# Map scatters and attention gathers of a four-model graph network: counted by batch with up to 96 open, and no scatters in the graph's pass

## The chip, the core and the metric

The kernel runs on one core of one Trainium2 chip. The metric is the device time of one execution in microseconds; lower is better. All arithmetic is float32.

## The reference

Node rows `x` (50,000 x 128) and 25,000 edges (`src`, `dst`, sorted by `dst`) go through four graph networks one after the other. Each adds its result to `x` and normalizes the row. The first one has four attention layers, and it is the one that the change touches:

```python
h = x @ W
e = ea @ We
alpha = (h @ a_s)[src] + (h @ a_d)[dst] + e @ a_e
alpha = leaky_relu(alpha, 0.2)
alpha = segment_softmax(alpha, dst, N)
out = segment_sum(h[src] * alpha[:, None], dst, N) + b
x = (out - mean(out)) * rsqrt(var(out) + 1e-5) * gamma + beta
```

After it come a relation network of three layers, a neighbour-mean network of three layers and one tensor-product convolution, all on the same edges.

## The kernel before

The work is a sequence of passes, each a `Pass` with its own tiles and semaphores. At the end of a pass all five engines meet, GpSimd clears the pass's semaphores, and they meet again (lines 76 to 79). So a pass lasts until its last engine is done, and nothing of the next one starts earlier.

The 25,000 edges are padded to 25,088 and stand in 196 columns (`K`) of 128 edges. A gather or scatter by edge moves 128 rows, one for each partition, and is one indirect DMA that GpSimd (POOL) issues. The passes that matter here:

- **graph** (lines 744 to 950) works out for each edge which segment it is in and where its row goes. VectorE and TensorE do it in a chain of small steps, ScalarE stores the second half of a map from nodes to rows, SyncE (SP) stores the results. POOL runs the first 24 of 196 map scatters (`EARLY`), which wait until the whole map has landed (`self_mapped`). A map scatter writes four floats for each edge that ends a segment into the table `gat_rows0`.
- **dense0**, named `x` in the trace (lines 966 to 1049), takes 98 blocks of 512 nodes. SP loads `x`, TensorE transposes and multiplies, VectorE completes the row, SP stores 536 KB a block into the same table, in columns that the map scatters don't write. POOL runs the other 172 map scatters beside it.
- **p0** (`PlainLayers` with `FirstRows`): POOL first gathers 196 columns by `dst` (line 2406, through a ring of four slots), then 196 columns by `src` into the big tile `H` (`gather_rows`, line 2358). Meanwhile all nodes run through attention layers 1 to 3 as if they had no edges on the other engines, in 98 blocks (the plain stream). VectorE ends with the logits.
- **p1, p2, p3** (`plain_rows`): `gather_rows` again brings 196 columns from that layer's table (132 floats a row), beside a plain stream that takes a third of the 98 blocks through the networks that follow. The logits stand at the start of these.
- **soft** and **d** (line 1145 on) follow each of p0 to p3 and read `H`. They need all 196 columns.

`place_in_map` and `gather_rows` count what they have open with sixteen semaphores: DMA number `c` adds to semaphore `c % 16`. Before each sixteenth DMA they wait on all sixteen, that is until every DMA issued so far has landed. At the end they wait on all sixteen again.

Of the kernel before, what the change touches and what calls it, by code (L numbers as in the profile page):

```python
# [8 lines left out]
U32 = mybir.dt.uint32  # L9
# [20 lines left out]
R_DST, R_SRC, R_TYPE, R_SH, R_LEN, R_TE = 0, 1, 2, 4, 8, 24  # L30
MUL = 32
PEEL = 10
RING = 16


class Chain:
# [289 lines left out]
class Kernel:  # L326
# [29 lines left out]
    def build(self):  # L356
# [17 lines left out]
        with ExitStack() as ctx:  # L374
# [16 lines left out]
            with ExitStack() as gat:  # L391
                self.rend = gat.enter_context(nc.sbuf_tensor("rend", [P, K], F32))
                self.asad = gat.enter_context(nc.sbuf_tensor("asad", [P, K, 2], F32))
                self.prev01 = gat.enter_context(nc.sbuf_tensor("prev01", [HALF, 2, P], F32))
                self.head01 = gat.enter_context(nc.sbuf_tensor("head01", [HALF, 2, P], F32))
                self.next01 = gat.enter_context(nc.sbuf_tensor("next01", [HALF, 2, P], F32))
                self.carry01 = gat.enter_context(nc.sbuf_tensor("carry01", [HALF, 2, P], F32))
                self.pen_row = gat.enter_context(nc.sbuf_tensor("pen_row", [1, 2, K], F32))
                self.row01 = gat.enter_context(nc.sbuf_tensor("row01", [1, 2, K], F32))
                self.Wg = gat.enter_context(nc.sbuf_tensor("Wg", [P, 4, TW], F32))  # L400
                self.cg = gat.enter_context(nc.sbuf_tensor("cg", [P, 4, TW], F32))
                self.Gc = gat.enter_context(nc.sbuf_tensor("Gc", [P, D], F32))
                self.g3 = gat.enter_context(nc.sbuf_tensor("g3", [P, D], F32))
                with Pass(nc, "early") as early:
                    self.b3, self.mapv = early.sb("b3", [P, D]), early.sb("mapv", [P, KG, KT, 4])
                    self.flag, self.own_i = early.sb("flag", [1, 1], I32), early.sb("own_i", [P, C], I32)
                    self.mput, self.placed = early.sb("mput", [P, K], U32), early.sems("map_placed", RING)
                    self.self_map, self.self_mapped = early.sb("self_map", [P, NP // P, 4]), early.sem("self_map_stored")
                    self.weights, self.plain_constants = Weights(self, early), PlainConstants(self, early)
                    self.records()  # L410
                    self.order()
                    self.graph()
                    self.dense0()
                self.H = gat.enter_context(nc.sbuf_tensor("H", [P, K, T0W], F32))
                self.lt = gat.enter_context(nc.sbuf_tensor("logit_terms", [P, 2, K], F32))
                self.pw = gat.enter_context(nc.sbuf_tensor("pw", [P, K], F32))
                self.pl = gat.enter_context(nc.sbuf_tensor("pl", [P, K], F32))
                self.te2 = gat.enter_context(nc.sbuf_tensor("te2", [P, K], F32))
                first = 0
                for l in range(4):  # L420
                    if l == 0:
                        self.run("p0", lambda q: PlainLayers(self, q), lambda q: FirstRows(self, q))
                    else:
                        self.plain_rows(l, first, (self.NBLK - first) // (4 - l))
                        first += (self.NBLK - first) // (4 - l)
                    with ExitStack() as marks:
                        self.same = marks.enter_context(nc.sbuf_tensor(f"same_run{l}", [P, ND], U8))
                        self.soft(l)
                        self.slots(l)
# [314 lines left out]
    def graph(self):  # L744
# [3 lines left out]
        with Pass(self.nc, "graph") as q:  # L748
# [20 lines left out]
            pr, pc = q.ps("rows", 4), q.ps("cols")  # L769
            ld, ch, sbr, sbst, icst = q.sem("loaded"), q.sem("steps"), q.sem("marks_ready"), q.sem("marks_stored"), q.sem("rows_stored")  # L770
            fr, ft, fk = q.sem("fields_ready"), q.sem("fields_turned"), q.sem("fields_kept")
            er, et, cr, ct, ohr, mr = (q.sem(n) for n in ("ends_ready", "ends_turned", "carries_ready", "carries_turned", "kinds_ready", "map_rows_ready"))
            block = q.block()
            by_row = lambda ap: ap.rearrange("(g r p) -> r g p", g=2, p=P)

            pt, pa, pc_ = pr[:, 0, :], pr[:, 1, :], pr[:, 2, :]

            @block.gpsimd
            def _(pool):
                pool.wait_ge(mr, 1)  # L780
                pool.wait_ge(self.self_mapped, 16 * (self.G + 1))
                self.place_in_map(pool, 0, self.EARLY)

            @block.scalar
            def _(act):
# [71 lines left out]
            def _(v):  # L857
# [37 lines left out]
                v.wait_ge(ft, 1)  # L895
                v.tensor_scalar(self.src2_i[:, :], pf[0][:, K:2 * K], 2.0, 1.0, ALU.mult, ALU.add)
                v.tensor_copy(self.dst_i[:, :], pf[1][:, 0:K])
                v.tensor_scalar(self.mput[:, :], pf[1][:, K:2 * K], float(2 * T0W // 4), float((GB + MAP) // 4), ALU.mult, ALU.add).then_inc(mr, 1)
                v.tensor_copy(self.put_i[:, :], pf[1][:, K:2 * K])
                st.run(v.tensor_copy(self.rend[:, :], pf[2][:, 0:K]))  # L900
                v.sem_inc(fk, 1)
# [48 lines left out]
                v.tensor_copy(self.shareD[:, :], pf[2][:, 0:K])  # L950


    EARLY = 24

    def place_in_map(self, pool, first, end):

        pieces = self.t0w.rearrange("n (q w) -> (n q) w", w=4)
        bound = pool.to_reg(self.NP * 2 * T0W // 4 - 1)
        for c in range(first, end):
            if c and c % RING == 0:  # L960
                for j in range(RING):
                    pool.wait_ge(self.placed[j], c // RING * 16)
            pool.indirect_dma_start(pieces, bass.IndirectOffsetOnAxis(self.mput[:, c:c + 1], 0), self.mapv[:, c // KT, c % KT, :], None,  # L963
                                    bounds_check=bound, oob_is_err=False).then_inc(self.placed[c % RING], 16)

    def dense0(self):

# [2 lines left out]
        with Pass(self.nc, "x") as q:  # L970
# [25 lines left out]

            @block.gpsimd
            def _(pool):
                self.place_in_map(pool, self.EARLY, K)
                for j in range(RING):  # L1000
                    pool.wait_ge(self.placed[j], len(range(j, K, RING)) * 16)

            @block.tensor
            def _(pe):
# [1343 lines left out]
def gather_rows(kn, pool, got, table, index, rows, width, before=()):  # L2348

    K, bound = kn.K, pool.to_reg(rows - 1)  # L2350
    for c in range(K):
        if c == K - 8 * KT:
            for s, n in before:
                pool.wait_ge(s, n)
        if c and c % RING == 0:
            for j in range(RING):
                pool.wait_ge(got[j], c // RING * 16)
        pool.indirect_dma_start(kn.H[:, c, 0:width], None, table, bass.IndirectOffsetOnAxis(index[:, c:c + 1], 0),  # L2358
                                bounds_check=bound, oob_is_err=False).then_inc(got[c % RING], 16)
    for j in range(RING):  # L2360
        pool.wait_ge(got[j], len(range(j, K, RING)) * 16)


class FirstRows(Stream):


    def __init__(self, kn, q):
# [1 line left out]
        self.dg = kn.H[:, kn.K - 8 * KT:kn.K, :].rearrange("p c w -> p (c w)").rearrange("p (r k w) -> p r k w", r=4, k=KT)  # L2369
        self.heads_kept, self.attr_kept = q.sem("heads_kept"), q.sem("attr_kept")  # L2370
        self.gate = q.sem("store_gate")
        self.dgot, self.dput, self.got = q.sems("slot_rows_in", 4), q.sems("slot_rows_stored", 4), q.sems("edge_rows_in", RING)
        self.logits = Logits(kn, q, 0)

    def sync(self, sp):
# [50 lines left out]
class Rows(Stream):  # L2426


    def __init__(self, kn, q, l, banks):
        self.kn, self.l = kn, l  # L2430
        self.got = q.sems("edge_rows_in", RING)
        self.logits = Logits(kn, q, l, banks)

    def sync(self, sp):
# [677 lines left out]
```

## Time and profile before

| | us |
|---|---|
| Median of 3 runs | 6403.81 (6377.07 to 6413.65) |
| Span of the profiled execution | 5398.9 |
| What the median has beside that span | 1004.9 |
| POOL busy in the span | 2893.9 (54%) |
| TensorE, VectorE, ScalarE busy | 3821.1, 3792.3, 3176.1 |

The span runs from the profiled execution's first engine instruction to its last. Its own time is known only as this span; the time around it is taken as the difference to the median. No engine is busy for more than 71% of the span, so the share of busy time doesn't name a bound: it has to be read pass by pass, from what each pass's end waits for.

### The profile page before, as it was taken

Reading aid. Unit: us, or ns where it says so; the run is one execution under the profiler, and the core shown is the slowest. Engines: PE = TensorE matmul, PEld = TensorE weight load, DVE = VectorE, ACT = ScalarE, POOL = GpSimd, SP = SyncE. Lnnn points to the kernel's source line nnn. Section 1 sums busy time; section 2 is a strip of 40 time slices with the busy share of each in tenths; the row PEclk is TensorE's granted clock in tenths of the full one; section 3 lists DMA queues with packets and bytes.
Section 4 is the critical chain, followed back from the end, with each engine's and each line's share of the span. In section 5 each row is a group of like instructions: output and inputs, shape, how many; then the busy total and the mean of one; then the engine's idle time right before and its main releaser. Section 6 shows DMA issues by size and latency. Waiting matters only on the chain. (4 is left out here: it accounts for less than half of the span.)

```text
span 5398.9 us, 104328 instructions
## 1 busy us (share of the span) xinstructions
PE 3821.1 (71%) x23663; PEld 3143.4 (58%) x23663; DVE 3792.3 (70%) x10843; ACT 3176.1 (59%) x11279; POOL 2893.9 (54%) x2759
## 2 busy tenths in 40 slices
PE   6355889566747685768575768678688787977775
PEld 5354778565537453645474545456577676866665
DVE  2575889688849784978596767677567675756666
ACT  2022889577848684868482323356577685655554
POOL 0466766603650463066205867676376564757776
PEclk8698999888979797979676767677799998988777
DMA  8898999556955694578463446555489797872221
GB/s 183 129 301 269 383 362 278 176 148 179 283 175 149 203 283 154 156 229 278 149 184 126 131 129 189 167 158 177 165 282 303 248 305 238 246 189 66 62 66 57
DMA packets 918273, 1074.23 MB, mean 199 GB/s; under 512 B 202780, under 2 KB 565066, under 8 KB 917107
## 3 DMA queue, kind: packets, MB, share of 16 engines
q1 hardware_dynamic: 763570, 890.24, 50.5%
q0 software_dynamic: 90944, 180.06, 13.6%
q10 hardware_dynamic: 63556, 1.81, 1.6%
q8 instruction: 56, 0.92, 0.1%
q14 instruction: 147, 1.20, 0.1%
HBM read 509.54 MB, written 566.14 MB: 199 GB/s over the span
## 5 line engine op out<-in xcount | busy, mean ns | idle before, releaser
L2358 POOL DMA_INDIRECT H<-gat_rows,src_i x784 | 804.1, 1026 | 1032.9 <-POOLq L79 620.9
L1909 POOL DMA_INDIRECT s_G<-sage_rows,src_i x588 | 602.4, 1025 | 369.6 <-issue 161.0
L1695 POOL DMA_INDIRECT r_G<-rel_rows,idx x392 | 441.7, 1127 | 216.8 <-issue 110.2
L1708 PE MATMUL r_t<-r_oh,relv 8*128 8x512 f32 x294 | 227.4, 862 | 217.5 <-issue 77.2
L2547 PE MATMUL p_M<-Wg,p_hT 128*128 128x132 f32 x2352 | 336.6, 287 | 63.1 <-DVE p_res L2604 48.8
L1743 ACT ACTIVATE r_mT<-r_t 128x512 f32<-128x512 f32 x147 | 87.4, 594 | 460.4 <-PE r_t L1711 460.1
L2547 PEld LDWEIGHTS p_M<-Wg,p_hT 128*128 128x128 f32 x2352 | 290.3, 192 | 113.0 <-issue 96.0
L2604 DVE SCALAR_TENSOR_TENSOR p_res<-p_M,p_rr,cg 128x132 f32<-128x132 f32 x1176 | 333.8, 346 | 2.5 <-PE p_M L2547 1.4
L1304 PE MATMUL d_S<-ones,d_sqT 128*128 128x1 f32 x1568 | 224.3, 264 | 144.0 <-DVE d_ve L1449 144.0
L2686 PEld LDWEIGHTS p_pl_p<-Wn,p_pl_h 128*128 128x128 f32 x1568 | 205.9, 198 | 201.8 <-ACT p_pl_h L2780 154.9
L2686 PE MATMUL p_pl_p<-Wn,p_pl_h 128*128 128x128 f32 x1568 | 225.3, 289 | 132.6 <-ACT p_pl_h L2780 132.4
L1304 PEld LDWEIGHTS d_S<-ones,d_sqT 128*128 128x128 f32 x1568 | 217.0, 214 | 172.2 <-issue 133.4
L1605 DVE TENSOR_TENSOR_SCAN r_agT<-same_run,r_agT,r_mT 128x512 f32<-128x512 f32 (+1 forms) x144 | 184.4, 1281 | 185.2 <-ACT r_mT L1743 185.1
L1711 PEld LDWEIGHTS r_t<-share_squares,r_G 128*128 128x128 f32 x1176 | 200.8, 258 | 160.5 <-issue 160.5
L963 POOL DMA_INDIRECT gat_rows<-early_mapv,early_mput x196 | 195.1, 995 | 168.8 <-DMA gat_rows<-early_self_map 57.6
L1695 POOL DMA_INDIRECT r_G<-n_rows,src_i x196 | 235.4, 1201 | 78.5 <-issue 54.2
L2119 POOL DMA_INDIRECT share_squares<-features,src_i x196 | 217.1, 1108 | 94.6 <-issue 58.6
L1353 ACT ACTIVATE d_hs<-d_hs,pl 128x128 f32<-128x128 f32 x784 | 248.4, 399 | 15.8 <-DMA d_hs<-gat_rows 11.9
L2406 POOL DMA_INDIRECT H<-gat_rows,dst_i x196 | 196.1, 1001 | 92.9 <-issue 48.9
L1443 DVE TENSOR_TENSOR_SCAN d_yT<-same_run,d_yT,d_T 128x512 f32<-128x512 f32 (+1 forms) x192 | 244.5, 1273 | 0.3 <-ACT d_sqT L1359 0.2
L2111 POOL DMA_INDIRECT out_dram<-tp_v,put_i x196 | 198.7, 1014 | 77.6 <-issue 56.7
L1711 PE MATMUL r_t<-share_squares,r_G 128*128 (+1 forms) x1176 | 236.6, 363 | 0.0
(482 smaller groups left out, 12286.0 us busy)
## 6 DMA issues: line engine op xcount, KB each, us to landing
gat_rows<-p_res SPq DMA_DIRECT2D x294, 264.0 KB
sage_rows<-p_pl_s SPq DMA_DIRECT2D x294, 256.0 KB
gat_rows<-x_row SPq DMA_DIRECT2D x98, 536.0 KB
gat_rows<-d_res SPq DMA_DIRECT2D x147, 264.0 KB
d_hs<-gat_rows SPq DMA_DIRECT2D x147, 256.0 KB
s_hT<-sage_slots_t SPq DMA_DIRECT2D x147, 256.0 KB
slot_rows<-H SPq DMA_DIRECT2D x49, 544.0 KB, 11.5
x_x<-in_x SPq DMA_DIRECT2D x98, 256.0 KB
```

The costliest lines, as they stand in the source:

```text
L1304: mm = pe.matmul(pS[:, k:k + 1], sqT[:, b.s2, k * P:(k + 1) * P], self.ones[:, :], start=True, stop=True)
L1353: last = act.activation(hs[:, b.s4, k, :], hs[:, b.s4, k, :], ACT.Copy, scale=self.pl[:, bass.ds(b.n * KT + k, 1)])
L1443: v.tensor_tensor_scan(yT[:, b.s4, :], self.same[:, bass.ds(b.n * BLOCK, BLOCK)], pT[b.s2][:, :], 0.0 if first else yT[:, (b.m - 1) % 4, B ...
L1695: pool.indirect_dma_start(self.G[:, g % 4, k, :], None, table, bass.IndirectOffsetOnAxis(index[:, c:c + 1], 0), bounds_check=bound, oob_is ...
L1708: pe.matmul(pt[:, :], kn.relv[:, l, :], self.oh[:, b.m % self.Y, :], start=True, stop=False)
L1711: mm = pe.matmul(pt[:, k * P:(k + 1) * P], self.G[:, b.s4, k, :], share, start=False, stop=(k == KT - 1))
L1909: pool.indirect_dma_start(self.G[:, g % 4, k, :], None, kn.st[self.l], bass.IndirectOffsetOnAxis(kn.idx[:, c:c + 1], 0), bounds_check=boun ...
L2119: pool.indirect_dma_start(self.G[:, c, :], None, kn.f, bass.IndirectOffsetOnAxis(kn.idx[:, c:c + 1], 0), bounds_check=bound, oob_is_err=Fa ...
L2358: pool.indirect_dma_start(kn.H[:, c, 0:width], None, table, bass.IndirectOffsetOnAxis(index[:, c:c + 1], 0), bounds_check=bound, oob_is_er ...
L2547: mm = pe.matmul(self.pM[self.bank(b, j)][:, k // 2, (k % 2) * TW:(k % 2 + 1) * TW], self.hT[l][:, b.s2, k * P:(k + 1) * P], kn.Wg[:, l, : ...
L2604: last = v.scalar_tensor_tensor(self.res[l][:, b.s4, k, :], self.pM[self.bank(b, j)][:, k // 2, (k % 2) * TW:(k % 2 + 1) * TW], self.rr[l] ...
L2686: mm = pe.matmul(bank[:, k * D:(k + 1) * D], xT[:, k * P:(k + 1) * P], w, start=True, stop=True)
```

## The change

Both loops use one semaphore for each batch of sixteen DMAs (thirteen in all, the last batch has four). The DMA that begins batch `b` waits only from `b = 5` on, and then only for batch `b - 5`. So at most five whole batches and the one being issued, 96 DMAs, are not yet known to have landed. The loop's end waits for all thirteen semaphores. The graph pass has no GpSimd part any more: all 196 map scatters stand in dense0, behind the same wait for the map.

```diff
-RING = 16
+BATCH = 16
+OPEN = 5
@@ in build; the gathers' semaphores "edge_rows_in" in FirstRows and Rows likewise
-                    self.mput, self.placed = early.sb("mput", [P, K], U32), early.sems("map_placed", RING)
+                    self.mput, self.placed = early.sb("mput", [P, K], U32), early.sems("map_placed", -(-K // BATCH))
@@ in graph
-            @block.gpsimd
-            def _(pool):
-                pool.wait_ge(mr, 1)
-                pool.wait_ge(self.self_mapped, 16 * (self.G + 1))
-                self.place_in_map(pool, 0, self.EARLY)
@@ place_in_map
-            if c and c % RING == 0:
-                for j in range(RING):
-                    pool.wait_ge(self.placed[j], c // RING * 16)
+            if c % BATCH == 0 and c >= OPEN * BATCH:
+                pool.wait_ge(self.placed[c // BATCH - OPEN], BATCH * 16)
             pool.indirect_dma_start(pieces, bass.IndirectOffsetOnAxis(self.mput[:, c:c + 1], 0), self.mapv[:, c // KT, c % KT, :], None,
-                                    bounds_check=bound, oob_is_err=False).then_inc(self.placed[c % RING], 16)
+                                    bounds_check=bound, oob_is_err=False).then_inc(self.placed[c // BATCH], 16)
@@ in dense0
             def _(pool):
-                self.place_in_map(pool, self.EARLY, K)
-                for j in range(RING):
-                    pool.wait_ge(self.placed[j], len(range(j, K, RING)) * 16)
+                pool.wait_ge(self.self_mapped, 16 * (self.G + 1))
+                self.place_in_map(pool, 0, K)
+                for j in range(-(-K // BATCH)):
+                    pool.wait_ge(self.placed[j], min(BATCH, K - j * BATCH) * 16)
@@ gather_rows
-        if c and c % RING == 0:
-            for j in range(RING):
-                pool.wait_ge(got[j], c // RING * 16)
+        if c % BATCH == 0 and c >= OPEN * BATCH:
+            pool.wait_ge(got[c // BATCH - OPEN], BATCH * 16)
         pool.indirect_dma_start(kn.H[:, c, 0:width], None, table, bass.IndirectOffsetOnAxis(index[:, c:c + 1], 0),
-                                bounds_check=bound, oob_is_err=False).then_inc(got[c % RING], 16)
-    for j in range(RING):
-        pool.wait_ge(got[j], len(range(j, K, RING)) * 16)
+                                bounds_check=bound, oob_is_err=False).then_inc(got[c // BATCH], 16)
+    for j in range(-(-K // BATCH)):
+        pool.wait_ge(got[j], min(BATCH, K - j * BATCH) * 16)
```

On POOL, the order from the graph pass to p0 was this before. Line 778 is the start of the graph pass's GpSimd part, line 997 that of dense0's; lines 76 and 78 are the end of a pass.

```order
L778 UNCONDITIONAL_BRANCH
L963 DMA gat_rows<-early_mapv,early_mput 3411968x4 x24
L76 UNCONDITIONAL_BRANCH
L78 ISA
L997 UNCONDITIONAL_BRANCH
L963 DMA gat_rows<-early_mapv,early_mput 3411968x4 x172
L76 UNCONDITIONAL_BRANCH
L78 ISA x2
L461 UNCONDITIONAL_BRANCH
L2406 DMA H<-gat_rows,dst_i 128x272 x196
L2358 DMA H<-gat_rows,src_i 128x136 x196
```

And with the change (whose lines are up to eight lower; 989 is dense0's part):

```order
L697 UNCONDITIONAL_BRANCH
L79 ISA x2
L989 UNCONDITIONAL_BRANCH
L955 DMA gat_rows<-early_mapv,early_mput 3411968x4 x196
L77 UNCONDITIONAL_BRANCH
L79 ISA x2
L462 UNCONDITIONAL_BRANCH
L2398 DMA H<-gat_rows,dst_i 128x272 x196
L2350 DMA H<-gat_rows,src_i 128x136 x196
L77 UNCONDITIONAL_BRANCH
```

The 24 scatters have moved past the end of the graph pass. Between the pass that orders the edges and dense0 POOL only meets the other engines.

Inside `gather_rows`, here that of p1 on POOL, every sixteenth row waited for sixteen semaphores before. A semaphore is named after its first use in the program, so that some of p1's carry names of earlier passes; the printout cuts the long rows.

```order
L461 UNCONDITIONAL_BRANCH [waits barrier_Pool_Activation_PE_DVE_SP_gather]
L2358 DMA H<-gat_rows,src_i 128x132 x16
L2358 DMA H<-gat_rows,src_i 128x132 [waits p0_edge_rows_in10,p0_edge_rows_in11,p0_edge_rows_in9,p0_edge_rows_in12,p0_edge_rows_in8,p0_edge_rows_in13,p0_edge_rows_in7,p0_edge_rows_in14,p0_edge_rows_in6,p0_edge_rows_in15,p0_edge_rows_in5,
L2358 DMA H<-gat_rows,src_i 128x132 x15
L2358 DMA H<-gat_rows,src_i 128x132 [waits p0_edge_rows_in10,p0_edge_rows_in11,p0_edge_rows_in9,p0_edge_rows_in12,p0_edge_rows_in8,p0_edge_rows_in13,p0_edge_rows_in7,p0_edge_rows_in14,p0_edge_rows_in6,p0_edge_rows_in15,p0_edge_rows_in5,
```

With the change the first eighty gathers stand without a wait, and each sixteenth one behind them names a single semaphore:

```order
L462 UNCONDITIONAL_BRANCH [waits barrier_Pool_Activation_PE_DVE_SP_gather]
L2350 DMA H<-gat_rows,src_i 128x132 x80
L2350 DMA H<-gat_rows,src_i 128x132 [waits p0_edge_rows_in2]
L2350 DMA H<-gat_rows,src_i 128x132 x15
L2350 DMA H<-gat_rows,src_i 128x132 [waits p0_edge_rows_in3]
```

The first wait has moved from behind 16 gathers to behind 80, and it asks for the batch that was issued 80 to 64 gathers before.

## Rows read from the trace of the kernel before

**Rows 1.** The page: the span, and three groups of its fifth part.

```profile
span 5398.9 us, 104328 instructions
...
L2358 POOL DMA_INDIRECT H<-gat_rows,src_i x784 | 804.1, 1026 | 1032.9 <-POOLq L79 620.9
L1909 POOL DMA_INDIRECT s_G<-sage_rows,src_i x588 | 602.4, 1025 | 369.6 <-issue 161.0
...
L963 POOL DMA_INDIRECT gat_rows<-early_mapv,early_mput x196 | 195.1, 995 | 168.8 <-DMA gat_rows<-early_self_map 57.6
```

**Rows 2.** Waits of POOL: instruction <- what ended them: us, times, longest us.

```profile
POOL H L2358 <- DMA H<-gat_rows,src_i: 197.9, 98, 5.5
...
POOL gat_rows L963 <- DMA gat_rows<-early_mapv,early_mput: 50.6, 23, 5.7
```

**Rows 3.** Timeline, POOL, map scatters: start, us, line, count, [idle before].

```profile
177.00 1.30 POOL L963 DMA_INDIRECT gat_rows<-early_mapv,early_mput  x1 [57.61 <-DMA gat_rows<-early_self_map]
...
213.28 0.97 POOL L963 DMA_INDIRECT gat_rows<-early_mapv,early_mput  x1 [3.65 <-POOLq L79]
```

**Rows 4.** Timeline, SP, the first of the dense pass.

```profile
212.54 0.34 SPq L992 DMA_DIRECT2D x_na<-in_node_vec  x1
```

**Rows 5.** DMA busy tenths, 40 slices of 0.9 us from 177 us.

```profile
DMA  0000277779996000000000000000000000000000
```

**Rows 6.** Windows: busy us of PE, PEld, DVE, ACT, POOL; clock, DMA, GB/s.

```profile
213.00:483.00 270.00, 155.73 (x1176) 137.39 (x1176) 194.94 (x686) 58.52 (x98) 170.77 (x172) 0.98 0.99 293
772.00:1030.00 258.00, 242.38 (x1923) 217.70 (x1923) 252.51 (x922) 229.54 (x838) 165.70 (x167) 1.00 0.90 279
1281.00:1550.00 269.00, 202.52 (x1091) 144.63 (x1092) 214.29 (x719) 209.85 (x479) 178.57 (x173) 0.91 0.84 258
```

**Rows 7.** Queue of POOL, 300 to 480 us: packets, MB, share of 16 engines.

```profile
q0 software_dynamic: 3584, 0.21, 1.7%
```

**Rows 8.** Timeline, all engines, the end of the dense pass.

```profile
482.24 1.11 POOL L963 DMA_INDIRECT gat_rows<-early_mapv,early_mput  x1 [0.30 <-issue]
493.69 0.41 SPq L2298 DMA_DIRECT2D p_terms<-logit_terms_of_edges  x1
```

**Rows 9.** DMA busy tenths, 40 slices of 0.375 us from 480 us.

```profile
DMA  9998107999699999100000000000000000000005
```

**Rows 10.** Timeline, all engines, the end of pass p0.

```profile
1035.93 0.36 DVE L2345 TENSOR_TENSOR logit_terms<-pw,pl 128x196 f32<-128x196 f32 x1
...
1072.95 1.00 POOL L2358 DMA_INDIRECT H<-gat_rows,src_i  x1 [0.30 <-issue]
1085.92 0.33 SPq L1167 DMA_DIRECT2D same_run<-same_as_before  x1
```

**Rows 11.** Timeline, all engines, the ends of p1, p2 and p3.

```profile
1552.56 1.69 SPq L2672 DMA_DIRECT2D plain_z_t<-p_pl_zT  x2
...
1584.92 1.00 POOL L2358 DMA_INDIRECT H<-gat_rows,src_i  x1 [0.30 <-issue]
1597.62 0.33 SPq L1167 DMA_DIRECT2D same_run<-same_as_before  x1
...
2073.53 1.32 SPq L2672 DMA_DIRECT2D plain_z_t<-p_pl_zT  x2
...
2111.06 0.33 SPq L1167 DMA_DIRECT2D same_run<-same_as_before  x1
...
2584.53 2.06 SPq L2672 DMA_DIRECT2D plain_z_t<-p_pl_zT  x2
...
2621.14 0.33 SPq L1167 DMA_DIRECT2D same_run<-same_as_before  x1
```

**Rows 12.** Timeline, all engines, end of d0, without gathers.

```profile
1277.72 0.33 SPq L1281 DMA_DIRECT2D gat_rows<-d_res  x1
...
1280.70 0.38 SPq L2298 DMA_DIRECT2D logit_terms<-logit_terms_of_edges  x1
```

**Rows 13.** Line 1695, gathers without landing waits: ns min/median/max, first, last.

```profile
L1695 POOL DMA_INDIRECT r_G<-n_rows,src_i x196: 996/1082/2162, 2877.0 to 3170.8; - x196
```

More of the change, by code:

```diff
@@ L771, in graph @@
             fr, ft, fk = q.sem("fields_ready"), q.sem("fields_turned"), q.sem("fields_kept")
-            er, et, cr, ct, ohr, mr = (q.sem(n) for n in ("ends_ready", "ends_turned", "carries_ready", "carries_turned", "kinds_ready", "map_rows_ready"))
+            er, et, cr, ct, ohr = (q.sem(n) for n in ("ends_ready", "ends_turned", "carries_ready", "carries_turned", "kinds_ready"))
             block = q.block()
@@ L897, in _ @@
                 v.tensor_copy(self.dst_i[:, :], pf[1][:, 0:K])
-                v.tensor_scalar(self.mput[:, :], pf[1][:, K:2 * K], float(2 * T0W // 4), float((GB + MAP) // 4), ALU.mult, ALU.add).then_inc(mr, 1)
+                v.tensor_scalar(self.mput[:, :], pf[1][:, K:2 * K], float(2 * T0W // 4), float((GB + MAP) // 4), ALU.mult, ALU.add)
                 v.tensor_copy(self.put_i[:, :], pf[1][:, K:2 * K])
@@ L950, in _ @@
                 v.tensor_copy(self.shareD[:, :], pf[2][:, 0:K])
-    EARLY = 24
     def place_in_map(self, pool, first, end):
@@ L2371, in __init__ @@
         self.gate = q.sem("store_gate")
-        self.dgot, self.dput, self.got = q.sems("slot_rows_in", 4), q.sems("slot_rows_stored", 4), q.sems("edge_rows_in", RING)
+        self.dgot, self.dput, self.got = q.sems("slot_rows_in", 4), q.sems("slot_rows_stored", 4), q.sems("edge_rows_in", -(-kn.K // BATCH))
         self.logits = Logits(kn, q, 0)
@@ L2430, in __init__ @@
         self.kn, self.l = kn, l
-        self.got = q.sems("edge_rows_in", RING)
+        self.got = q.sems("edge_rows_in", -(-kn.K // BATCH))
         self.logits = Logits(kn, q, l, banks)
```

## The prediction

> **What bounds the kernel now.** I read the program pass by pass, since engines meet at the end of each. The page first: POOL is idle for 1032.9 us before the gathers of line 2358 and for 168.8 us before the map scatters [rows 1]. Most of the first figure are passes that have no gathers. What the change can reach is in the view of waits: 98 waits of gathers on gathers, 197.9 us, the longest 5.5, and 23 of scatters on scatters, 50.6 us [rows 2]. The reader must take the ordinary pace off these. Two indirect DMAs in a row stand 0.30 us apart with nothing to wait for [rows 8, 10]. So 197.9 - 98 x 0.30 = 168.5 us of real waiting in the four passes, 42.1 us in each. For the scatters it is 50.6 - 23 x 0.30 = 43.7 us.
>
> Then, for each pass, who ends last. Dense0: the DMA engines are busy for 0.99 of the stretch, and no engine more than 195 of 270 us [rows 6], so the DMAs pace it. The last scatter ends at 483.35, the last data move at 480 + 17 x 0.375 = 486.4, and the next pass starts at 493.69 [rows 8, 9]. p0: VectorE ends at 1036.3, POOL at 1073.95, the next pass starts at 1085.92 [rows 10]. p1: SP's last issue ends at 1554.25, POOL ends at 1585.92, the next pass starts at 1597.62; in p2 and p3 SP ends at 2074.85 and 2586.59, and the next passes start at 2111.06 and 2621.14 [rows 11]. So in p0 to p3 POOL alone keeps the pass open, for 30 to 40 us.
>
> One more thing stands in these rows. After the last gather a pass needs another 12 us. In d0, where POOL has no DMAs, the next pass starts 3.0 us after the last store is issued [rows 12]. Landing is some 3 us of the 12, so about 9 us are POOL's own closing of a pass with many indirect DMAs. I take it that POOL does this as soon as its own list is done, while the others still work.
>
> **The change, part by part.**
>
> *The graph pass.* Its DMAs are done at 177 + 13 x 0.9 = 188.7 [rows 5], and POOL's scatters, begun at 177.00, keep it open until the next pass at 212.54 [rows 3, 4]. Without them the pass should end about 1.5 us after the last data: dense0 starts at 190.2, 22.3 us earlier.
>
> *Dense0.* The 24 scatters come in here. POOL's queue takes 1.7% of the DMA engines from 300 to 480 us [rows 7]. I take that share for the whole stretch: 4.6 us for 172 scatters [rows 6], 0.027 us each, so 0.6 us for 24; I take 1. On POOL 196 scatters at 0.995 + 0.30 us are 253.8 us. From 190.9 they end at 445, and with 10.3 us of landing and closing at 455. The dense stream ends at 486.4 - 22.3 + 1 = 465.1. So POOL drops out of this pass's end, and its closing is hidden: the next pass starts 1.5 us after the last data instead of 7.3 us, 5.8 us less. Together 22.3 - 1 + 5.8 = 27.1 us. If POOL weren't earlier than the stream, only 21 would be left.
>
> *p0.* POOL waits 42.1 us less: the gathers end at 1031.9 and the pass at 1043.8. VectorE's end at 1036.3 would allow 1037.8, so POOL still bounds it, by 6 us. VectorE is busy for 252.5 of 258 us here [rows 6], which means that more DMA traffic has little to delay. Gain 42.1; the bounds are 35 (below) and 48 (were POOL not last).
>
> *p1 to p3.* POOL's own end would come 42.1 us earlier, at 1555.5, 2069.0 and 2579.0. But the plain streams don't move. After SP's last issue I allow 4 us, a little over the 3.0 of d0, since stores still queue there: 1558.3, 2078.9, 2590.6. These are later, so they bound the passes. Gains 39.4, 32.2 and 30.5, 102.1 together.
>
> *What the streams pay.* All gathers now fall beside the plain stream. In p1 that is 196 instead of 173 [rows 6], 23 more of 128 x 132 x 4 bytes, 1.55 MB. At the stretch's 258 GB/s this is 6.0 us if the DMAs bound the stream, and nothing if they don't. The DMA share is 0.84, VectorE is busy for 80%: mixed. I take 2 us for each of the three, 6 in all (0 to 18). In p0 29 more gathers of 69.6 KB are 7 us at 279 GB/s, inside the margin of 6 but for 1.
>
> *A gather's own time.* It is 1.026 us in the mean with the waits between batches, and 1.025 us in 588 gathers of line 1909, which wait for a slot and never for the landing of sixteen [rows 1]. So I see no price for leaving out the waits. The one wait in sixteen that is left asks for a batch issued 64 x 1.33 = 85 us before. The waits of now end at most 5.5 us after a batch's last issue, so it is met on arrival.
>
> The Trainium skill has a rule on those waits. "DMA: Bandwidth & Descriptors", section "Anatomy of one DMA — SWDGE (gpsimd) path", gives about 2 us fixed from issue to landing. By it the 48 waits (twelve in each pass) would cost 96 us. The rows show (197.9 - 50 x 0.30) / 48 = 3.8 us for each, under traffic [rows 2]; the trace's figure is used.
>
> **Sum.** 27.1 + 42.1 + 102.1 - 6 = 165.3 us. Against the profiled execution: a span of 5398.9 - 165.3 = 5233.6 us. What the median has beside it, 1004.9 us, is taken as unchanged, so 6403.8 - 165.3 = 6238.5, say 6238 us. The three runs spread from 6377 to 6414, so about 0.5% (32 us) is what can be told from no change.
>
> **The rivals.**
>
> *Closing in the open* (9%). If POOL's closing begins only when every engine is done, the 5.8 us of dense0 are lost and p1 to p3 end some 9 us later each. 165.3 - 5.8 - 27 = 132: 6271 us. For it: in every pass of the trace where POOL ends last it can't be told apart. Against it: nothing yet but the order of the instructions.
>
> *The streams are stretched* (10%). If the faster gathers cost each plain stream 12 us instead of 2, and p0 7 beyond its margin, 165.3 - 30 - 7 = 128: 6275 us. It takes twice the bound by bytes.
>
> *Gathers slow down when nothing holds them* (7%). Those of line 1695 never wait for landings, and 195 intervals take 3170.8 - 2877.0 = 293.8 us, 1.51 us each instead of 1.33 [rows 13]. With 0.18 us more for each, POOL's ends in p0 to p3 come 35 us later than above and each pass gains 7 instead of 30 to 42. Dense0 gains 3 by its scatters' new end, against 22.3 of the start already in that figure. In all 31: 6373 us. For it: that row. Against it: line 1909, and p0, where beside the busiest VectorE 167 gathers take 165.70 us, 0.99 each [rows 6]. The Trainium skill has a reason for such a slowing: "SBUF — State Buffer", "SBUF: two separate sides", says that some VectorE operations lock GpSimd out while it writes descriptors. By that rule p0, with VectorE at 98%, should show long gathers, and the trace doesn't agree.
>
> *The waits only move* (3%). If DMAs landed more slowly than POOL issues them, 80 more would be open and then the pace would be the old one. Only the graph pass's 22 us would be gained: 6382 us. Against it: no wait in 98 is over 5.5 us [rows 2], and a backlog of sixteen would show as more.
>
> *Slower than before* (5%). Each gather blocks POOL itself when many are open, because the room for their descriptors runs out. The longest of line 1695 takes 2.16 us [rows 13]. At 1.40 instead of 1.03 us a pass's 196 gathers take 73 us more and lose 31 net: 124 in four passes. Dense0 would end at 190.9 + 196 x 1.67 + 10.3 = 528.5, 35 late. Together 159: 6563 us. It decides from 42.1 / 196 = 0.21 us more for each gather. Against it: a landing takes under 5.5 us, so that only four or five DMAs are open at a time, whatever is allowed.
>
> **How the numbers follow.** The forecast holds 66%. Its own range is 6210 to 6275: the streams' 0 to 18 us, p0's 35 to 48, and the spread of the medians. With the next two rivals, both inside that range or at its edge, that is 85%; I set 6195 to 6310. Faster by over 0.5%: 66 + 9 + 10 and half of the third rival, 88%. Within 0.5%: the other half and the fourth, 7%. Slower: 5%.
>
> **What the profile after would show.** Right: the first SP issue of dense0 near 190 us; scatters 1.3 us apart from first to last, ending near 445; gathers without gaps over 2 us, but for one or two; p0 about 42 us shorter; p1 to p3 ending 3 to 4 us after SP's last issue, with POOL done before it; gathers of 1.03 us. Wrong: gathers of 1.2 us or more; long gaps at each sixteenth gather from the sixth batch on; a plain stream that ends over 10 us later against its start; 9 us between SP's last landing and the next pass.

## The result and the profile after

The changed kernel takes 6722.86 us (6705.26 to 6731.76, 4 runs), the kernel before, beside it, 6396.47 us (6377.07 to 6413.65, 4 runs): a ratio of 1.0497, interval 1.0473 to 1.0521, 5% slower. The prediction was 6238 us with a range of 6195 to 6310.

The page of the changed kernel, the lines that answer to [rows 1]:

```profile
span 6717.3 us, 103836 instructions
...
L2350 POOL DMA_INDIRECT H<-gat_rows,src_i x784 | 787.8, 1005 | 1567.0 <-POOLq L80 1308.5
```

The span is 6717.3 us and the execution's own time 6719.09, so 1.8 us lie beside the span. So the changed kernel has nothing like the 1004.9 us that the prediction carried along unchanged. A second profile of the kernel before has its own page:

```profile
span 6379.1 us, 104328 instructions
...
L2358 POOL DMA_INDIRECT H<-gat_rows,src_i x784 | 798.8, 1019 | 1382.7 <-POOLq L79 1027.8
```

Its span is again its whole time (6380.9 us). The first trace of before, with 5398.9 us, shows an execution that wasn't like those that were timed. None of 58 later timings of that kernel was under 6363 us, and what made that one execution shorter stays open; the 1004.9 us are the difference between two unlike executions. Below, "before" is the second trace.

The changed kernel's waits of POOL, its first SP issue of dense0, and its last scatter:

```profile
POOL H L2350 <- POOLq L80: 1308.5, 3, 450.8
...
POOL H L2350 <- issue: 237.6, 780, 0.3
```

```profile
188.11 0.34 SPq L984 DMA_DIRECT2D x_na<-in_node_vec  x1
```

```profile
438.27 0.97 POOL L955 DMA_INDIRECT gat_rows<-early_mapv,early_mput  x1 [0.30 <-issue]
```

So POOL did what the prediction said, but for one thing. Of the 98 waits on landings [rows 2] none is left, 780 of the 784 gathers stand 0.3 us behind the last one, three open a pass, dense0 starts 22 us earlier, and the last scatter ends at 439 (predicted: 445). The 784th is gather 164 of p0: it waits 21.0 us for ScalarE's copy of the slot rows (`naD`, line 2384), for which POOL didn't have to wait before. The other engines are the surprise. Windows of the changed kernel (columns as in [rows 6]): dense0 with the scatters, their end and what follows, and then p1's gathers and what follows them:

```profile
230.00:280.00 50.00, 2.98 (x12) 2.58 (x12) 4.00 (x14) 0.60 (x1) 38.12 (x40) 0.50 0.08 18
280.00:330.00 50.00, 5.97 (x24) 5.16 (x24) 2.00 (x7) 1.19 (x2) 38.12 (x40) 0.50 0.12 34
...
430.00:480.00 50.00, 12.64 (x68) 11.07 (x68) 14.04 (x50) 4.07 (x7) 7.11 (x8) 0.59 0.29 90
480.00:530.00 50.00, 31.15 (x240) 27.29 (x240) 39.65 (x140) 11.94 (x20) 0.00 (x0) 1.00 1.03 323
1780.00:2042.00 262.00, 43.12 (x132) 27.63 (x132) 47.41 (x160) 33.05 (x76) 198.03 (x196) 0.53 0.35 88
2042.00:2260.00 218.00, 169.59 (x958) 121.75 (x958) 168.12 (x559) 176.34 (x402) 0.00 (x0) 0.96 0.65 221
```

While POOL issues without a break, PE does 12 to 24 matmuls in 50 us; from 480 us on, 40 us behind the last scatter, it does 240. In between the streams recover slowly. In p1 the stream has 132 of its 1090 matmuls done when the gathers end, and does the other 958 in 218 us. The pass is nearly a sum of POOL's list and the stream, no longer a maximum. The timeline of the changed kernel shows what the engines wait for, here in one block of dense0 (all engines; rows between these are left out; with "remote" or "issue" the profile can pin the end of a wait on no instruction):

```profile
257.55 1.06 PE L1002 MATMUL x_T<-ident,x_x 128*128 128x128 f32 x4
...
276.68 0.77 DVE L1031 TENSOR_TENSOR x_row<-x_M,cg 128x264 f32<-128x264 f32 x2 [31.57 <-issue]
...
277.58 1.13 DVE L1039 SCALAR_TENSOR_TENSOR x_row<-x_x,x_row,early_b 128x128 f32<-128x128 f32 x4
278.74 0.33 SPq L978 DMA_DIRECT2D x_x<-in_x  x1
...
288.58 0.60 ACT L1019 ACTIVATE x_xT<-x_T 128x512 f32<-128x512 f32 x1 [33.00 <-remote]
```

By the profile PE ends its transposes into x_T at 258.61, and ScalarE's copy, for which all else had long been done, starts at 288.58, 30 us later. VectorE starts 19 us after the product that it adds to (ended at 257.76). The other steps of the block follow at once: SP issues 0.03 us after VectorE's last instruction, and PE starts at 289.23, 0.05 us after ScalarE's. So what comes late in dense0 is what PE has to report. (Ends of matmuls are modelled in a profile, so it can't tell a late report from a matmul that really ends late.) And the DMA engines, in tenths over 40 slices of 5 us from 230 to 430 us:

```profile
DMA  0005000000500000320000050000005000000400
```

They are idle but for one burst in some 33 us, so it isn't traffic that holds the streams up. The bursts stand in the slices in which SP issues, or the next (the load of 278.74 in the one from 280): SP's transfers aren't late, their issue is. TensorE's granted clock is 0.50 in these windows, the level of 1.2 GHz, and 1.00 (2.4 GHz) from 480 on. In the block above PE's work takes 3.2 us at the lower clock (2.13 and 1.06), out of 33.6 us from block to block: the lower clock comes with the stall, and isn't its cause.

### The profile page after: what moved, and what is told of

Same layout as the page of the kernel before. It is cut to its first block and busy times, and to the rows that moved or that the text cites. A ratio compares the mean times of both kernels' runs of the same rounds, so it can differ in the third digit from the quotient of the medians.

```text
span 6717.3 us, 103836 instructions
## 1 busy us (share of the span) xinstructions
PE 3967.6 (59%) x23663; PEld 3257.4 (48%) x23663; DVE 3804.8 (57%) x10843; ACT 3177.4 (47%) x11279; POOL 2874.0 (43%) x2759
## 5 line engine op out<-in xcount | busy, mean ns | idle before, releaser
L2350 POOL DMA_INDIRECT H<-gat_rows,src_i x784 | 787.8, 1005 | 1567.0 <-POOLq L80 1308.5
L2539 PE MATMUL p_M<-Wg,p_hT 128*128 128x132 f32 x2352 | 371.3, 307 | 283.7 <-issue 150.3
L2539 PEld LDWEIGHTS p_M<-Wg,p_hT 128*128 128x128 f32 x2352 | 326.3, 212 | 327.8 <-issue 297.0
L2569 ACT ACTIVATE p_hT<-p_T 128x512 f32<-128x512 f32 x294 | 173.0, 588 | 424.3 <-remote 352.2
L1019 ACT ACTIVATE x_xT<-x_T 128x512 f32<-128x512 f32 x98 | 58.4, 597 | 488.7 <-remote 222.7
L1711 PE MATMUL r_w<-Wr,r_agT 128*128 128x128 f32 x1176 | 234.1, 365 | 72.5 <-issue 39.2
L1009 PE MATMUL x_M<-Wg,x_xT 128*128 128x132 f32 x784 | 116.7, 297 | 236.6 <-issue 171.5
L1711 PEld LDWEIGHTS r_w<-Wr,r_agT 128*128 128x128 f32 x1176 | 217.2, 276 | 80.4 <-issue 47.0
```

The source lines that it names most:

```text
L1711: mm = pe.matmul(self.pw[b.s2][:, k * P:(k + 1) * P], self.agT[:, b.m % self.Y, k * P:(k + 1) * P], kn.Wr[:, l, :], start=True, stop=True)
L2539: mm = pe.matmul(self.pM[self.bank(b, j)][:, k // 2, (k % 2) * TW:(k % 2 + 1) * TW], self.hT[l][:, b.s2, k * P:(k + 1) * P], kn.Wg[:, l, : ...
```

## The experiments

"Theory" is from here on: while POOL issues indirect DMAs without a break, updates of semaphores between the other engines and DMA completions come late. (The block above bears it out for PE's updates alone.) In the second trace of before, dense0 shows the same in small. POOL waits there for sixteen landings until 223.13 us, and these are the 10 us windows behind that wait:

```profile
226.00:236.00 10.00, 5.99 (x45) 5.17 (x45) 5.03 (x18) 1.79 (x3) 7.56 (x9) 0.97 0.94 274
236.00:246.00 10.00, 2.19 (x9) 1.48 (x8) 0.09 (x1) 0.03 (x1) 6.56 (x7) 0.50 0.24 79
```

The streams run for some 13 us behind the pause, and then they stand.

The runs were made on several chips, on which the kernel before takes 6386 to 6545 us, so each is set beside the timings of before on its own chip. An expectation in us leans on times from another chip and can be 1 to 2% off for that alone.

**before_again, move_only, gathers_only, open2.** The kernel before once more; the scatters all in dense0, with the old waits; only `gather_rows` changed; and the changed kernel with `OPEN = 2`.

> The kernel before, unchanged, for a trace whose span answers to its time. The first trace has a span of 5398.9 us where the median is some 1000 us more, while the changed kernel's span of 6717 is its time. Stalled-stream theory (while POOL issues indirect DMAs back to back, semaphore updates and transfers of the others come tens of us late; each pause of POOL lets them catch up): a span near 6390, with the missing 1000 us in the passes in which POOL issues many DMAs (dense0, p0 to p3, r, s, tp), and none in soft and d. Rival, time outside the engines' work (a start or an end that the span leaves out): a span of 5400 again.

> The kernel before with all 196 scatters in dense0, still in batches of sixteen that wait for each other; gathers unchanged. Stalled-stream theory: the graph pass is 22 us shorter, dense0 about 25 to 40 us longer, since its pauses stay: the same to 0.5% slower, 6380 to 6430. Rival, the scatters in dense0 are the trouble by their place: dense0 near 500 us and a time near 6600.

> The kernel before with only the gathers of p0 to p3 counted by batch with OPEN 5; scatters unchanged. Stalled-stream theory: p1 to p3 take 480 to 500 us each as in the changed kernel (gathers and plain stream one after the other), p0 near 890: most of the loss, a time of 6600 to 6700 if the kernel before has spent part of it already. Rival, the loss is in dense0: p1 to p3 as before and a time near 6400.

> The changed kernel with OPEN 2: a batch waits for the one before the last, so up to 32 are open. A landing takes about 4 us and a batch 21, so this wait is met on arrival and POOL doesn't pause. Stalled-stream theory: as slow as with OPEN 5, 6700 to 6740. Rival, the number of open DMAs does it (96 or 80 fill a queue, 32 don't): near or below the kernel before, 6250 to 6400.

Measured beside 6386.12 us of before: 6380.9 (one look); 6402.2, ratio 1.003 (1.0004 to 1.0056); 6670.4, 1.0454 (1.042 to 1.0488); 6716.9, 1.0539 (1.0503 to 1.0576). All four came out as their theory had it. The place of the scatters brings nothing: the graph's pass gives 23 us and dense0 takes 32 (463 to 495). Nearly all of the loss is the gathers' missing waits, and how many DMAs may be open doesn't matter: with `OPEN` at 2 (32 open at most; at 5 the code admits 80, not the title's 96) every wait is met on arrival too, and the time is the same. Since neither limit is ever reached, this run says nothing of what many DMAs really open at once would do.

**ring8, ring4: shorter batches.** The kernel before with one line changed.

```diff
-RING = 16
+RING = 8        # ring4: 4
```

> The kernel before with its ring of sixteen cut to eight, so that POOL pauses for the landings after every eighth indirect DMA (24 waits of some 2.2 us in a pass of 196 instead of 12). Stalled-stream theory (while POOL issues indirect DMAs one after the other the other engines hardly get on; each pause lets them catch up): POOL's own time in a pass grows by 12 x 2.2 = 26 us, but what is left of the plain stream behind it (about 120 us in p1 to p3 of before) shrinks by 60 to 90. p1 to p3 take 350 to 380 us instead of 400 to 410, dense0 420 to 450 instead of 463; in all 6280 us (6150 to 6340). Rival (a pass is the sum of POOL's list, with its waits, and the stream's rest, and pauses buy nothing): 5 x 26 = 130 us more, 6520 us.

> The same with a ring of four: 48 waits in a pass. Stalled-stream theory: POOL's list grows to 257 + 48 x 2.1 = 358 us, and the plain stream (210 us without POOL's DMAs) fits wholly into it: p1 to p3 about 360 us instead of 400 to 410, dense0 about 380 to 420 instead of 463; in all 6150 us (6000 to 6300). Rival (pauses buy nothing): 36 more waits of 2.1 us in each of five passes, 6386 + 378 = 6760 us.

Measured beside 6474.9 us: 6104.95, ratio 0.9422 (0.9382 to 0.9462), and 6264.55, 0.968 (0.9661 to 0.9698). More waits, less time: the rival, by which waits only add, is out. ring8 is 45 us under its expected range, ring4 is 115 over its value, inside its range. A wait for four landings took 2.3 to 5.4 us and not 2.1, so in ring4 POOL's list (398 us in p1) bounds the pass again.

**pause16, pause4, pause8, pause4x1, pause2x1, pause4x2: pauses without waits.** The changed kernel, whose waits for landings are all met, with fills of a scratch tile ahead of the DMAs:

```diff
+def pause(pool, idle, sem, c):
+    if c and c % EVERY == 0:
+        for j in range(PARTS):
+            pool.memset(idle[:, :], 0.0).then_inc(sem, 1)
+            pool.wait_ge(sem, (c // EVERY - 1) * PARTS + j + 1)
...
     for c in range(K):
+        pause(pool, kn.idle, got[-1], c)
```

> The changed kernel (96 may be open) with POOL filling a scratch tile of 256 columns five times, each fill waited for, after every sixteenth indirect DMA: some 2.5 us without a DMA and without any wait for a landing. Stalled-stream theory (it is the lack of pauses in POOL's issue): the other engines get on in the pauses as they did in the waits, so the time comes back to that of the kernel before, less the 22 us of the graph pass: 6370 us (6300 to 6480). Rival (it is the number of open DMAs, or the waits for landings themselves): no gain from pauses, 6723 + 5 x 12 x 2.5 = 6870 us.

> As pause16, but three fills after every fourth indirect DMA, some 1.5 us each. Stalled-stream theory: 48 pauses make POOL's list 257 + 72 = 329 us; if the streams get on for most of the pauses' time and a little after each, p1 to p3 end near 340 us and the whole near 6150 us (6000 to 6350). If only the length of a pause counts, and 1.5 us is too short to let a late update through, it is as slow as the changed kernel or slower: 6700 to 7000 us. Rival (number of open DMAs): 6723 + 5 x 72 = 7080 us.

Measured beside 6474.9 us: pause16 6586.4, ratio 1.0167 (1.0112 to 1.0222), and pause4 5901.96, 0.9114 (0.9095 to 0.9134). POOL does more work and waits for nothing new but its own fills, and the kernel is 9% faster than before and 13% faster than the changed one (0.9114 / 1.0497 = 0.868). That is the decisive run: a pause helps without any landing waited for, and POOL being busy with fills does no harm as long as it isn't issuing DMAs. pause16 falls between theory and rival, 106 us over the theory's range, of which its chip explains most (6480 x 6474.9 / 6386.1 = 6570). It is 3% faster than the changed kernel, but not back at before's time: its pauses are 1.9 us long, shorter than before's waits of 2.4. In the trace of pause4 a pause looks like this (the next gather starts at 1604.52), and p1 now ends 12 us behind the last gather, as in [rows 11]:

```profile
1602.18 1.00 POOL L2362 DMA_INDIRECT H<-gat_rows,src_i  x1 [0.31 <-issue]
1603.18 1.07 POOL L42 MEMSET idle<- 128x256 f32 x3
```

```profile
1441.00:1757.00 316.00, 199.62 (x1100) 141.91 (x1100) 215.51 (x720) 210.23 (x480) 250.68 (x340) 0.88 0.75 229
```

The window is p1's gathers: all 1100 matmuls of the stream lie in it.

> As pause4, with the three fills after every eighth indirect DMA: 24 pauses of 1.04 us, 25 us in a pass. By the sum of the pauses (pause16: 20 us and p1 at 451; pause4: 50 us and p1 at 328) p1 comes out near 430 us, in all 6450 us (6300 to 6550). If how long POOL issues without a break counts (eight in a row instead of sixteen or four), it lies nearer pause4: p1 340 to 370, in all 6050 us (5950 to 6200).

> As pause4 with one fill after every fourth indirect DMA in place of three: 48 pauses in a pass that are some 0.4 us longer than the ordinary 0.30 us (pause4: 1.04 us longer). If it is the number of pauses that lets the streams go on, POOL's list falls from 307 to 275 us and p1 to p3 with it, from 328 to 300 us; dense0 and p0 gain too, in all about 5760 us (5700 to 5880). If the sum of the pauses counts (17 us here, 20 in pause16, 50 in pause4), it is as pause16: 6550 us (6400 to 6650).

> One fill after every second indirect DMA: 97 pauses of about 0.4 us, 34 us in a pass, POOL's list 291 us. If short runs are what counts: p1 to p3 at 310 us, in all 5820 us (5750 to 5900). If a pause has to have some length, over 0.4 us, to let anything through: as the changed kernel, 6700 us or more. By the sum of the pauses alone (34 us, between pause16 and pause4): 6250 us.

> Two fills after every fourth indirect DMA, 48 pauses of 0.7 us, 33 us in a pass. The runs so far give, by the sum of the pauses in a pass: 17 us p1 481, 20 us 451, 26 us 417, 29 us 428 (and 409 in before), 51 us 328. On that line 33 us give p1 about 395 and the whole 6200 us (6100 to 6330). If three fills are a threshold (a pause has to reach 1 us), 6450 us or more; if two are enough, POOL's list of 291 us bounds the pass, p1 310 and the whole 5800 us.

Measured: beside 6498.8 us, pause8 6492.4, ratio 0.9989 (0.996 to 1.0019); pause4x1 6702.9, 1.0289 (1.0243 to 1.0335); pause2x1 6410.4, 0.9845 (0.9802 to 0.9888). Beside 6545.1 us, pause4x2 6322.95, 0.9667 (0.9628 to 0.9706). pause4x1 shows that 48 pauses of 0.4 us bring little: 2% under the changed kernel (1.0289 / 1.0497), and 53 us over even the range that the sum of the pauses gave them. But it isn't that a pause of under 0.4 us does nothing: the 97 shorter ones of pause2x1 take 6% off the changed kernel. pause2x1 lies between the sum's value (6250) and the threshold's, pause8 and pause4x2 are where the sum puts them.

**pause16x12, pause8x6: the sum of pause4 in longer pieces.**

> The sum of pause4 (50 us in a pass) in few long pieces: twelve fills, some 4.2 us, after every sixteenth indirect DMA. If the sum of the pauses decides, p1 to p3 last as long as POOL's list, 328 us, and the whole 5900 us (5850 to 5980). If what a pause releases is bounded by the work that stands ready when it begins (pause16: 12 pauses of 1.7 us and some 5 us of stream for each), long pauses bring little more than short ones: p1 near 450, 6500 us or more.

> Six fills, some 2.1 us, after every eighth indirect DMA: pause4's and pause16x12's sum (51 to 54 us in a pass) in pieces of middle size. Backlog theory: what POOL's issue holds up first piles up unseen for some 10 us (eight DMAs; in pause16x12 the other engines ran on to 1760, 11 us behind a pause, and then stood), and each DMA needs about 0.25 us of pause to drain. Then eight DMAs with 2.1 us are never held up: p1 to p3 end with POOL's list, 328 to 345 us, in all 5900 to 6000 us. By the mere number of pauses (24, half of pause4's) it lies half way between pause16x12 and pause4: p1 375, in all 6160 us.

Measured: 6420.8 beside 6545.1, ratio 0.9816 (0.9783 to 0.985), and 6076.0 beside 6493.3, 0.9343 (0.9307 to 0.938). pause16x12 lies between its two values, 440 us over the range of the sum's, so the sum alone doesn't decide. Windows of pause16x12, where POOL's fills run from 1744.23 to 1748.62:

```profile
1755.00:1760.00 5.00, 3.77 (x20) 2.46 (x20) 4.53 (x14) 2.70 (x6) 3.78 (x5) 1.00 0.95 284
1760.00:1765.00 5.00, 0.00 (x0) 0.00 (x0) 0.56 (x5) 0.11 (x1) 3.84 (x4) 0.89 0.33 89
```

The streams run on for 11 us and stand again. pause8x6 should, by the picture of a backlog that takes eight DMAs to build, have been as pause4; it is 76 us over the upper end of that, and 84 under the interpolation. My reading is that the hold-up sets in by degrees; no run shows that by itself. All runs in one table. It is worked out from the traces, as means of p1 to p3: a pass from the end of the one before to its own, POOL's list from its first gather's start to the last one's end, a pause beyond the ordinary 0.30 us, and the stream's work behind the list. The traces come from several chips, so that differences of a few us mean nothing.

| kernel | pauses: number x us | list us | pass us | pass less list us |
|---|---|---|---|---|
| changed | 0 | 257 | 494 | 237 |
| pause4x1 | 48 x 0.4 | 274 | 486 | 212 |
| pause16 | 12 x 1.9 | 281 | 452 | 171 |
| pause8 | 24 x 1.1 | 285 | 427 | 141 |
| pause2x1 | 97 x 0.3 | 289 | 424 | 136 |
| before | 12 x 2.4 | 290 | 406 | 116 |
| pause16x12 | 12 x 4.4 | 313 | 420 | 108 |
| pause4x2 | 48 x 0.7 | 295 | 375 | 81 |
| pause8x6 | 24 x 2.2 | 315 | 356 | 41 |
| ring8 | 24 x 2.5 | 322 | 358 | 36 |
| pause4 | 48 x 1.1 | 316 | 328 | 12 |

By the last column the pauses of pause4 free 225 us of stream for 59 us more of POOL's list, 3.8 us for each. In most rows it is 2.7 to 4.1; it is 2.3 in pause16x12 and 1.5 in pause4x1. So the sum of the pauses goes far, and few long ones or very short ones behind every fourth DMA fall short of it. The 12 us left are landing and the closing of the pass.

**pause_all, best, best_early, ring16_pause4.** Pauses in every gather of the program; only where they pay; that with 24 scatters back in the graph's pass; and the kernel before, waits kept, with pause4's pauses.

```diff
 # best, in the slot rows of p0 and in the last pass; pause_all also in r and s
+            rest(self, pool, g)
             for k in range(KT):
```

> pause4 with the same pauses (three fills, of 192 columns) after every fourth indirect DMA of all the other gathers too: the slots' rows in p0, the gathers of the r and s passes and of the last pass. Stalled-stream theory: these passes too are longer in the runs than in the first trace of before, by 5 to 10 us each in r, 30 to 49 in s, 100 in the last pass; pauses bring part of that back: p0 700 instead of 742, s passes 345 instead of 370, the last 600 instead of 659; in all 5750 us (5650 to 5880). Rival (POOL waits for slots in these passes anyway, and its waits already are the pauses; more of them only add): 0 to 50 us slower than pause4, 5900 to 5960 us.

> pause4 with the pauses (three fills after every fourth indirect DMA) also in p0's gathers of slot rows and in the last pass, but not in the r and s passes, where pause_all measured them at a loss. By its passes, p0 gives 50 us and the last pass 40 us over pause4: 5902 - 90 = 5812 us (5770 to 5860). If what a pass gained there was given back in the ones behind it, 5900 us.

> The same with 24 map scatters back in the graph's pass. With pauses dense0 lasts as long as POOL's list (196 scatters, 315 us); 24 fewer take 24 x 1.30 + 6 x 1.04 = 37 us off it, and the graph's pass gets about 28 us longer: 9 us faster than best, 5803 us. If dense0 falls onto the bound of its stream first (270 us in the first trace of before), no more than that can be lost: 5812 to 5820 us. If the place of the scatters were worth what the prediction gave it (22 us), 5834 us.

> The kernel before, its waits for sixteen landings and its 24 scatters in the graph's pass kept, with the pauses of pause4 put in. Where the streams get on, POOL's list bounds the passes, and the waits cost what the prediction took for them less the pause that stands ahead of each: twelve in each of five passes at 1.1 to 2.4 us, 65 to 145 us, less 9 for the scatters' place: about 5990 us (5950 to 6040), 90 us over pause4. If the waits are free once there are pauses (or the changed counting is what hurt and not the missing pauses), 5895 us or less.

Measured: pause_all 5902.0 beside 6498.8, ratio 0.9061 (0.9014 to 0.9107). It gains 50 us in p0 and 40 in the last pass as its theory had it, but loses 46, 20, 21 and 21 in r0, r1, s0 and s1, and r2 and s2 bring only 6 and 12: the rival's time. In r0 POOL waited for nothing in pause4 but once, and its list gets 46 us longer (301 to 347), as the pass does. In r1, s0 and s1 it waited for slots in 12 to 42 places, and the pauses add 20 to 31 us to its lists all the same. best 5821.4 beside 6526.2, 0.8915 (0.8892 to 0.8938): 11% under before, the fastest found together with best_early, 5816.4, 0.8909 (0.8886 to 0.8933). Between these two the difference can't be told. By their passes the graph's gets 22 us longer and dense0 15 shorter, so the scatters' place is worth little either way. dense0 lasts 314 us in best and 504 in the changed kernel.

ring16_pause4: 5997.1 beside 6526.2, 0.919 (0.916 to 0.922), as expected. best met its expectation too. best_early came out at its second value, but not for its reason, a dense0 down at 270 us: dense0 lasts 299. ring16_pause4's p1 to p3 take 349 us and pause4's 328, its p0 752 and 742. Where the streams get on, taking out the waits brings what they last beyond the pause: 20 us in each of p1 to p3.

## Why the prediction was wrong

**The step that failed** stands under "p1 to p3": "But the plain streams don't move", with "I take 2 us for each of the three, 6 in all (0 to 18)" under "What the streams pay". In p1 to p3 the plain streams end 78, 97 and 87 us later against their start (passes before 409, 400, 410; changed 487, 496, 497), not 2. POOL's list did get 290 - 257 = 33 us shorter, and the work behind it 237 - 116 = 121 us longer. The step ahead of it failed too, "So in p0 to p3 POOL alone keeps the pass open": in the second trace of before POOL's last gather ends 109 to 119 us before the passes p1 to p3 do, and 214 before p0 does. The stream bounds them, and a shorter list alone could win nothing there. Over the program, p1 to p3 get 262 us longer, dense0 41 (463 to 504), p0 39 (854 to 894), and the graph's pass 23 shorter: 262 + 41 + 39 - 23 = 319 us of the 338 by which the spans differ. The other 19 lie in passes that the change doesn't touch, and no run says whether they are more than scatter. The bound of 0 to 18 us came from bytes over bandwidth. It priced DMA traffic, and the DMA engines are busy for only 0.08 to 0.13 of dense0's stall and 0.35 of p1's. Nothing in the prediction let the waits that it took out be of use to the other engines.

**The reason behind it** is one sentence of the sum: "What the median has beside it, 1004.9 us, is taken as unchanged." A sixth of the time stood in no row. In the second trace it is inside the passes: dense0 463 us instead of 281, p0 854 instead of 592, p1 to p3 400 to 410 instead of 317, the last 656 instead of 562, and the s passes 354 to 371 instead of 295 to 323. The three r passes, which have indirect DMAs too, differ by only 1 to 16 us. Every pass without indirect DMAs is the same in both (d0 180, the short ones 15). So nearly all of the missing time lay in passes with indirect DMAs, and most of it in the five in which the change works.

**POOL's side held.** 22.3 us were given to the graph's pass and 23 measured. A gather was to stay at 1.03 us, and is at 1.005. 42.1 us of waiting were to go from each of four passes; in the second trace the real waiting was 27 to 32 us, since the 98 waits of the first trace weren't typical either, and all of it went, though in p0 the new wait of 21 us took most of it back. The closing in cover can be seen as well, in p1, where POOL is done 229 us before the pass. SP's last issue and the first of the next pass, by the timeline:

```profile
2263.21 1.29 SPq L2664 DMA_DIRECT2D plain_z_t<-p_pl_zT  x2
...
2267.80 0.33 SPq L1160 DMA_DIRECT2D same_run<-same_as_before  x1
```

That is 3.3 us (3.2 in p2 and p3), inside the predicted 3 to 4 and not the 12 us behind a last gather.

**The rivals.** These 3.3 us refute the closing in the open (6271 us). Time lost in stretched streams was among them (6275 us), but at 12 us for a pass, and priced by traffic too. The one on the other side (6563 us) had POOL blocked by its own open DMAs. The gathers are no longer than before (1005 ns, 1019), and that refutes it. None had the mechanism that came. Of "what would show it wrong", one line did: a plain stream ending over 10 us later against its start.

**The rule that the prediction used.** The Trainium skill gives about 2 us from issue to landing ("DMA: Bandwidth & Descriptors", section "Anatomy of one DMA — SWDGE (gpsimd) path"). The gathers of pause4 come near it, with a median of 2.6 us from issue to landing; those of the first trace of before have 4.0, under traffic:

```profile
DMA to landing us min/median/max: 2.6/2.6/3.3
```

The Trainium skill's section "SWDGE vs HWDGE vs iDMA" on the same page says that DMAs issued from SP don't use the path by which VectorE can lock GpSimd out of writing descriptors, and so are immune to that. It speaks of another interference. Here the data of SP's DMAs move right behind the issue, but SP issues only once in 33 us while GpSimd issues, since what SP waits for is late; so being safe from that lock doesn't keep SP's stream going.

**What stays open.** That the streams stand while POOL issues without a break, and that pauses free them, is shown by the runs. That what PE reports comes late is shown in dense0, as far as a profile with modelled ends of matmuls can show it; where it queues isn't, nor whether reports of other engines or of landed DMAs come late elsewhere. Why the first execution had hardly any of this with the same program isn't known. Nor is it known whether scatters of 16 bytes a row cost less than gathers of 528 (both stall the streams: dense0 and p1).

## What to carry to other kernels

When a trace's span and the timed median differ by more than the passes can explain, no sum made on that trace is safe. Take the profile again, or ask in which passes the missing time could be, before pricing anything. A long list of indirect DMAs on POOL beside other streams has to be spaced: here a pause of 1 us after every fourth, in the 1.3 us pace, made the kernel 9% faster than waits for landings after every sixteenth did. The same pauses cost 20 to 46 us in four of six other passes. A wait that looks like pure idleness on one engine may be what lets the others run, so take a wait out together with a run that puts the bare pause back.

## What the runs showed of the hardware

- While POOL issues indirect DMAs 0.3 us apart, the other engines learn late of what PE has finished, in dense0 of the changed kernel by 19 us (VectorE) and 30 us (ScalarE). From ScalarE to PE and from VectorE to SP it takes 0.03 to 0.05 us in the same stretch, and SP's transfers start right behind their issue.
- The hold-up needs some 10 us of such issue to show fully (11 us in pause16x12, 13 in before) and goes within a pause of 1 us if only four DMAs went ahead of it. Behind 196 scatters without a break the streams took some 40 us to get going again. Pauses of 0.4 us after every fourth DMA bring 2%, pauses of 0.3 us after every second 6%.
- It isn't the traffic: DMA share 0.08 to 0.13 in dense0's stall, 0.35 beside p1's gathers. It isn't POOL's being busy: 3 fills in a row do no harm. And the limit on open DMAs plays no part (32 or 80: 6717 and 6723 us), since it is never reached.
